# Attention output through per-head values and output weights in place of per-head value maps, in a gated cross-attention and expert block

## The reference, cut to what matters

```python
# x (4, 1024, 256) f32, context (4, 154, 192), 8 heads of 64
def attention(x, context, mask, W_q, W_k, W_v, W_o, b_o):
    q = (x @ W_q).reshape(b, n, 8, 64)
    k = (context @ W_k).reshape(b, 154, 8, 64)
    v = (context @ W_v).reshape(b, 154, 8, 64)
    sim = where(mask, einsum('bihd,bjhd->bhij', q, k) * 64 ** -0.5, max_neg)
    attn = softmax(sim, axis=-1)
    out = einsum('bhij,bjhd->bihd', attn, v).reshape(b, n, 512)
    return out @ W_o + b_o

x = x + tanh(g_xattn) * attention(layernorm(x), ...)
h = layernorm(x)
# router: 32 experts in 8 groups, the best 4 groups, the best 6 experts, weights normalised
moe = sum over the 6 experts e of weight_e * (relu(h @ up_e.T) ** 2 @ down_e.T)      # inner size 128
shared = relu(h @ shared_up.T) ** 2 @ shared_down.T                                   # inner size 512
x = x + tanh(g_ffn) * (moe + shared)
```

## Time and profile before

| | us |
|---|---|
| median of 3 runs (lowest, highest) | 1016.27 (1015.75, 1018.07) |
| profiled execution, its own time | 1015.22 |
| its span, first to last instruction | 1013.4 |
| preparation, to the first score | 0 to 63.36 |
| slots, to the last `attn_out` | 63.36 to 440.68 |
| shared experts and last routing | 440.68 to 583.03 |
| experts and final sums | 583.03 to 1013.4 |

### The profile page before, as it was taken

One profiled execution on the slowest core, in us unless ns is written; L12 is line 12 of the kernel. 1 busy time (PEld: TensorE's weight loads), 2 busy tenths in 40 slices (PEclk: granted clock), 3 DMA queues, 4 the chain that ended last, 5 costly groups with the idle time before them and its releaser, 6 DMA issues.

```text
span 1013.4 us, 16914 instructions
## 1 busy us (share of the span) xinstructions
PE 828.7 (82%) x4985; PEld 680.9 (67%) x4985; DVE 496.7 (49%) x1574; ACT 380.0 (38%) x1120; POOL 497.3 (49%) x471
## 2 busy tenths in 40 slices
PE   5879999988888898949569987988877777877873
PEld 3668888777777787625345776777766666766753
DVE  1753368586767567634411132233333465645546
ACT  1235655444444454322113143434333333343330
POOL 2112114585858585846470035554545556656551
PEclk9999999999999999989688999899989999999986
DMA  9600000122412321244155045444544789878768
GB/s 313 206 1 1 1 1 23 58 85 65 181 62 80 110 93 51 93 174 159 62 179 168 23 137 156 143 149 140 164 143 152 244 252 298 267 236 268 239 218 316
DMA packets 76712, 144.66 MB, mean 143 GB/s; under 512 B 12624, under 2 KB 57936, under 8 KB 76112
## 3 DMA queue, kind: packets, MB, share of 16 engines
q1 hardware_dynamic: 51040, 63.89, 20.8%
q0 software_dynamic: 19968, 56.52, 15.0%
q10 hardware_dynamic: 5616, 23.16, 7.4%
HBM read 73.80 MB, written 69.73 MB: 142 GB/s over the span
## 4 chain that ended last, share of the span: by engine, by line
PE 55%; DVE 14%; another core or an unknown queue 13%; issue 9%; ACT 3%; DVEq 3%; DMA 2%; POOL 0%; POOLq 0%; SPq 0%; ACTq 0%
PE ps L1224 9%; PE ps L1245 8%; PE ps L1052 5%; PE ps L1111 4%; PE ps L1208 4%; PE ps L954 4%; PE ps L1004 3%; PE ps L1099 3%; PE ps L1039 3%; PE ps L977 2%; PE ps L1234 2%; PE ps L965 2%; DVE nmax L662 1%; PE ps L995 1%
## 5 line engine op out<-in xcount | busy, mean ns | idle before, releaser
L398 POOL DMA_INDIRECT token_parts<-hid,place x224 | 221.7, 990 | 236.7 <-ACT hid L550 173.7
L385 POOL DMA_INDIRECT routed_rows<-x_n,slots x144 | 144.7, 1005 | 67.8 <-issue 41.1
L1224 PE MATMUL ps<-big,att 128*128 x896 | 131.7, 293 | 43.1 <-ACT att L536 24.5
L1052 PE MATMUL ps<-big,att 128*128 128x256 f32 x640 | 146.5, 382 | 9.9 <-ACT att L463 8.0
L1224 PEld LDWEIGHTS ps<-big,att 128*128 128x128 f32 x896 | 116.2, 202 | 56.8 <-issue 54.0
L1245 PE MATMUL ps<-big,att 128*128 x448 | 125.3, 405 | 26.3 <-ACT att L542 24.0
L1052 PEld LDWEIGHTS ps<-big,att 128*128 128x128 f32 x640 | 118.4, 190 | 28.5 <-ACT att L463 10.8
L536 ACT ACTIVATE att<-ps 128x512 f32<-128x512 f32 x112 | 67.1, 600 | 157.3 <-remote 74.3
L883 DVE TENSOR_SCALAR att<-ps 128x256 f32<-128x256 f32 x112 | 47.6, 425 | 148.5 <-PE ps L1224 87.9
L1245 PEld LDWEIGHTS ps<-big,att 128*128 128x128 f32 x448 | 81.3, 202 | 38.5 <-issue 31.4
L378 POOL TENSOR_TENSOR att<-att,rsum 128x1232 f32<-128x1232 f32 x22 | 49.5, 2249 | 94.5 <-DVE rsum L667 94.3
(11 more groups left out here) (195 smaller groups left out, 1264.4 us busy)
## 6 DMA issues: line engine op xcount, KB each, us to landing
mid<-routed_rows SPq DMA_DIRECT2D x224, 138.0 KB
big<-token_parts ACTq DMA_DIRECT2D x19, 768.0 KB
x_n<-token_parts ACTq DMA_DIRECT2D x9, 768.0 KB
routed_rows<-pad_row SPq DMA_DIRECT2D x1, 4416.0 KB
routed_rows<-pad_row SPq DMA_DIRECT2D x32, 138.0 KB
big<-in_w_moe SPq DMA_DIRECT2D x1, 4352.0 KB, 12.7
x_all<-in_x SPq DMA_DIRECT2D x4, 1024.0 KB, 13.3
token_parts<-hid,place POOLq DMA_INDIRECT x224
```

Of the source, the lines that this page charges most:

```text
L385: nc.gpsimd.indirect_dma_start(rows, bass.IndirectOffsetOnAxis(ap=slots[:, t, k:k + 1], axis=0), normed(t), None).then_inc(s_sca[b % 3], 16)
L398: nc.gpsimd.indirect_dma_start(parts, bass.IndirectOffsetOnAxis(ap=place[:, p // 2 % 4, p % 2 * 2 + j:p % 2 * 2 + j + 1], axis=0), y_sb[:, ...
L1052: ins = M(ps[:, 7, 0:D], prob_t[:, c * P:(c + 1) * P], maps_u[b][:, c, :], start=c == 0, stop=c == NCH - 1)
L1224: ins = M(ps[:, 2 + p % 2, j * P:(j + 1) * P], xt[:, p % 2, j * 256 + c * P:j * 256 + (c + 1) * P], w_exp[:, bass.ds(e, 1), c * P:(c + 1) ...
```

## The change

The maps are gone. Preparation now computes keys (8 groups) and, for each batch entry, the values `v_all[b]` in three groups: for each of the 10 chunks of 128 (head, context row) pairs and each head that has rows in it, a block of 64 columns. There are 17 such (chunk, head) pairs. The context is kept in a buffer with zeros around each entry (`ctx_w`), so that rows of other heads come out as zero. ScalarE multiplies the output weights with the gate's tanh once.

In a slot the output of a tile takes three steps: `heads_out` (17 matmuls with 64 columns, into bank 7), `scale_heads` on VectorE (the inverse of the sums, multiplied in while the 512 values leave the bank), and, a slot later, `heads_t` (4 transposes), a copy by ScalarE (`save_heads_t`), and `attn_out` (4 matmuls with 256 columns). GpSimd no longer scales anything; it adds the output bias to x. The loops have 35 slots, not 34. Queries are computed two tiles ahead, in two parts. The second norm's rows are written by ScalarE (`norm_out`), from a scale and a shift by VectorE. The first norm's statistics are computed for 8 tiles in preparation and for the other 24 inside slots 0 to 5. `normed_2_t`, `logits` and `ranks` come one or two slots later. Of the experts' weights, 20 to 31 are loaded during preparation and 0 to 19 after the last `attn_out`.

```diff
-            for T in range(NT + 11):
-                if T >= 11:
-                    scatter(T - 11)
+            def add_bias(T):
+                pool.wait_ge(s_xn1, T + 1)
+                nc.gpsimd.tensor_tensor(x_all[:, T, :], x_all[:, T, :], bias_o[:], ALU.add).then_inc(s_xb, 1)
+            for T in range(NT + 14):
                 if T < NT:
-                    normalise(T)
+                    add_bias(T)
+                if T >= 14:
+                    scatter(T - 14)
...
+            def scale_heads(T):
+                dve.wait_ge(s_avp, T + 1)
+                V.reciprocal(rsum[:, T % 2, :], esum[:, T % 4, :])
+                dve.drain()
+                if T >= 1:
+                    dve.wait_ge(s_atp, T)
+                V.tensor_tensor(att_o.rearrange("p (h d) -> p h d", h=NH), ps[:, 7, :].rearrange("p (h d) -> p h d", h=NH),
+                                rsum[:, T % 2, :].unsqueeze(2).broadcast_to([P, NH, DH]), ALU.mult).then_inc(s_scl, 1)
...
-            for T in range(NT + 2):
+            for T in range(NT + 3):
+                if T >= 3:
+                    scale_heads(T - 3)
...
+                    base = CHUNK_AT[V_GROUPS[n][0]]
+                    for ch in range(*V_GROUPS[n]):
+                        for i, h in enumerate(CHUNK_HEADS[ch]):
+                            at = CHUNK_AT[ch] - base + i * DH
+                            win = P + ch * P - h * J
+                            for c in range(2):
+                                ins = M(ps[:, bank, at:at + DH], ctx_w[:, c, b, win:win + P], wv[:, c, h * DH:(h + 1) * DH],
+                                        start=c == 0, stop=c == 1, skip_group_check=True)
...
+            def heads_out(T):
+                b = T // (NT // NB)
+                slot = T + 2
+                if T >= 1:
+                    pe.wait_ge(s_at, T)
+                if slot % 4 == 0 and slot >= 8:
+                    pe.wait_ge(s_x2t, 2 * ((slot - 8) // 4) + 1)
+                if slot % 4 == 1 and slot >= 9:
+                    pe.wait_ge(s_le, (slot - 9) // 4 + 1)
+                pe.wait_ge(s_pt, 3 * T + 3)
+                for c in range(NCH):
+                    for i, h in enumerate(CHUNK_HEADS[c]):
+                        at = CHUNK_AT[c] + i * DH
+                        ins = M(ps[:, 7, h * DH:(h + 1) * DH], prob_t[:, c * P:(c + 1) * P], v_all[b][:, at:at + DH],
+                                start=c * P <= h * J, stop=(c + 1) * P >= (h + 1) * J, skip_group_check=True)
+                ins.then_inc(s_avp, 1)
+            def heads_t(T):
+                pe.wait_ge(s_scl, T + 1)
+                for m in range(MC):
+                    ins = nc.tensor.transpose(ps[:, 7, m * P:(m + 1) * P], att_o[:, m * P:(m + 1) * P], ident)
+                ins.then_inc(s_atp, 1)
...
             def attn_out(T):
+                pe.wait_ge(s_at, T + 1)
...
-                for c in range(NCH):
-                    if c % 4 == 0:
-                        pe.wait_ge(s_pt, 3 * T + c // 4 + 1)
-                    ins = M(ps[:, 7, 0:D], prob_t[:, c * P:(c + 1) * P], maps_u[b][:, c, :], start=c == 0, stop=c == NCH - 1)
+                for m in range(MC):
+                    ins = M(ps[:, 5, 0:D], att_t[:, m * P:(m + 1) * P], wo[:, m, :], start=m == 0, stop=m == MC - 1)
                 ins.then_inc(s_av, 1)
...
-            for i, (a, b, tiles) in enumerate(((0, EARLY_1, 16), (EARLY_1, EARLY_2, 24), (EARLY_2, NE, 32))):
-                sp.wait_ge(s_av, tiles)
-                sp.dma_start(w_exp[:, a:b, :], w_moe[:, a:b, :]).then_inc(s_we[i], 16)
+            sp.dma_start(w_exp[:, EARLY:NE, :], w_moe[:, EARLY:NE, :]).then_inc(s_we[0], 16)
+            sp.wait_ge(s_av, NT)
+            sp.dma_start(w_exp[:, 0:EARLY, :], w_moe[:, 0:EARLY, :]).then_inc(s_we[1], 16)
```

More of the change, by code:

```diff
@@ L948, in normed_1_t, with queries @@
                 ins.then_inc(s_x1p, 1)
-            def queries(T):
+            def queries(T, part):
                 pe.wait_ge(s_x1t, T + 1)
-                for m in range(MC):
+                for m in (2 * part, 2 * part + 1):
                     for c in range(KC):
@@ L1077, in ranks @@
                 pe.wait_ge(s_sel, b + 1)
+                pe.wait_ge(s_x1, min(TB * b + 9, NT))
                 if b >= 1:
@@ L1131, in down_late @@
                 ins.then_inc(s_dn2, 1)
-            for T in range(NT + 2):
+            for T in range(NT + 3):
+                if T == NT + 1:
+                    for s in range(3):
+                        up(0, s)
+                if 2 <= T < NT + 2:
+                    probs_t(T - 2, 0)
+                    probs_t(T - 2, 1)
                 if T < NT:
                     scores_0(T)
-                elif T == NT + 1:
-                    for s in range(3):
-                        up(0, s)
-                if T >= 2:
-                    probs_t(T - 2, 0)
+                if T + 2 < NT:
+                    normed_1_t(T + 2)
                 if T < NT:
                     scores_1(T)
-                if T + 1 < NT:
-                    queries(T + 1)
-                if T >= 2:
-                    probs_t(T - 2, 1)
+                if T >= 3:
+                    heads_t(T - 3)
+                if 2 <= T < NT + 2:
                     probs_t(T - 2, 2)
+                if T + 2 < NT:
+                    queries(T + 2, 0)
+                if T >= 3:
+                    attn_out(T - 3)
                 if T % 4 == 0 and T >= 8:
-                    logits((T - 8) // 4)
-                if T >= 2:
-                    attn_out(T - 2)
+                    normed_2_t((T - 8) // 4, 0)
+                if T % 4 == 1 and T >= 9:
+                    logits((T - 9) // 4)
                 if T + 2 < NT:
-                    normed_1_t(T + 2)
-                if T % 4 == 3 and T >= 7:
-                    normed_2_t((T - 7) // 4, 0)
-                    normed_2_t((T - 7) // 4, 1)
-                if T % 4 == 1 and T >= 9:
-                    ranks((T - 9) // 4)
+                    queries(T + 2, 1)
+                if T % 4 == 0 and T >= 8:
+                    normed_2_t((T - 8) // 4, 1)
+                if 2 <= T < NT + 2:
+                    heads_out(T - 2)
+                if T % 4 == 3 and T >= 11:
+                    ranks((T - 11) // 4)
             up(0, 3)
+            ranks(6)
             normed_2_t(7, 0)
@@ L1195, in _ @@
             pe.wait_ge(s_row, 1)
-            for i in range(3):
+            for i in range(2):
                 pe.wait_ge(s_we[i], 16)
```

317 lines of the change are left out of this document (158 added, 159 removed).

## The result

| | before | after |
|---|---|---|
| median, us (lowest, highest; 4 runs each) | 1016.01 (1012.98, 1018.07) | 1131.41 (1128.97, 1138.79) |
| profiled execution, its span | 1013.4 | 1137.0 |
| mean granted TensorE clock | 0.941 | 0.889 |

The ratio is 1.115, 95% interval [1.11, 1.12]: slower by 115 us. The forecast was 1037 (+21), with 1014 to 1060 as its range; the sign was right and the size wrong.

The account below looks back on a forecast made before the run. TensorE was taken as the bound, busy 828.7 of 1013.4 us. Slots 3-7 +8.2, slots 8-31 +16.7, slots 0-2 -6.5, the end +11.6 and preparation -9.0 sum to +21.0, so 1037 us, range 1014 to 1060.

Parts of the forecast that it names:

- Slots 8 to 31: Routing slots: TensorE's work grows by 1.64 us a slot, waits fall from 28.5 to 7 us, +16.7 us in all.
- the 28.5 us of waits: Slots 8 to 31 of before: TensorE's idle time, 1.2 us a slot, taken as waits for other engines.
- Rival 1: Slots 8 to 31: the new cross-engine chain costs what the old waits did, 21 us more, 1058 us; chance 0.18.
- The price of the new matmuls: TensorE's 64-column float32 matmuls in `heads_out`: 0.214 us each, a floor set by two weight loads.
- Rival 3: 64-column matmuls: columns alone count, so each takes 0.108 us and the kernel 965 us; chance 0.04.
- Preparation and slots 0 to 7: Preparation 44.1 us, -9.0; slots 0 to 2 about 20 us, -6.5; slots 3 to 7 +8.2.
- The end: Behind slot 31: +15.9 us if the old hole recurs, +7.4 if not; the middle, +11.6, was taken.
- the hole of 8.5 us: End of before: VectorE waits until 449.02 though the last `attn_out` starts before 440.68; cause not in the trace.
- Rival 2: Shared-expert stretch: TensorE's 23.4 us of "issue" holes and the end's hole all go, 1009 us; chance 0.12.

Follow-up runs that it names:

- e6_plain_writes: Kernel before with four bursts of 18 plain writes issued by SyncE in slots 4, 7, 10 and 13: 846.66 us, ratio 1.000 to before at 847.
- e9_after_again: Kernel after, unchanged, run again on a chip where before took 850 us: 894.42 us, ratio 1.056 to before.
- e14_train_again: Kernel before without GpSimd's scaling of the probabilities and without a wait between tiles' row writes: 832.38 us, ratio 0.984 to before.

## Why the prediction was wrong

Lengths in us of each stretch, a slot counted from its first mask row; "no holes" takes `e6_plain_writes` as before and `e9_after_again` as after.

| | forecast difference | result: before, after | no holes: before, after |
|---|---|---|---|
| start to first score | -9.0 | 63.4, 59.2 (-4.2) | 63.0, 59.5 (-3.4) |
| slots 0-2 | -6.5 | 26.5, 18.8 (-7.7) | 27.0, 18.8 (-8.2) |
| slots 3-7 | +8.2 | 48.1, 54.9 (+6.9) | 48.1, 54.9 (+6.9) |
| slots 8-30 | +16.7 with slot 31 | 269.4, 369.9 (+100.6) | 243.1, 273.6 (+30.4) |
| slot 31 to block 7's transposes | +11.6 without slot 31 | 47.1, 75.8 (+28.7) | 40.1, 57.6 (+17.5) |
| shared stretch | 0 | 128.7, 129.8 (+1.0) | 93.8, 99.1 (+5.4) |
| experts | 0 | 430.4, 428.7 (-1.7) | 328.6, 329.4 (+0.7) |

- **Slots 8 to 31: the step that failed.** The +16.7 was made of 291.4 us of work and 7 us of waits, in place of 28.5. Measured, for one slot less, are 316.1 us of busy TensorE and 53.8 of idle: +100.6. Two readings in that step were wrong.
- **First, the scaling was counted only as work whose removal frees a wait.** That it also parted the tiles of row writes stands in no term and no rival. With it gone they form trains of 18 and 24, and slots 8 to 30 lose 100.6 - 30.4 = 70 us more than without holes. That a train does this is shown by putting it into before (1.114) and spacing it again on the same chip (1.042). For after the evidence is 1.070 in place of 1.115 when paced, on another chip. That the chip or the job has its part is shown by the same two kernels at 0.984 and 1.051.
- **Second, the 28.5 us of waits weren't there to win.** They were taken as other engines in TensorE's way, which the change would free. Without holes before has 243.14 - 235.99 = 7.2 us of them over 23 slots, so there was little to win: +30.4, not +16.7. That most of the 28.5 was a milder form of the same disturbance is inferred, not shown: of the 26.2 us in before's slots 8 to 30 only 1.8 are "issue", and most name ScalarE, VectorE or "remote"; but VectorE's and ScalarE's own "issue" time there falls from 9.4 and 12.4 us to 2.4 and 0 without holes. The new chain of waits costs next to nothing: after has 3.5 us (273.56 - 270.08).
- **Even without holes the forecast misses.** 1.056 is above the 1060/1016 = 1.043 that ended its range. The waits are the largest part of that; the later start, the shared stretch (+5.4) and the end are the rest. There nearly the whole result is TensorE's own work: its busy time grows from 782.2 to 828.6, by 46.4 us, and the span by 49.3 (of two chips; side by side the medians are 45 and 46 us apart). Rival 1's +42 lies near it, but by luck: its mechanism isn't there.
- **The price of the new matmuls: right.** 0.221 us against 0.214 forecast, slot 10.99 against 11.1. Rival 3 (columns alone) is out. By the rule of the Trainium skill (TensorE: Matmul & The Clock Gate, LDWEIGHTS) that a weight load takes its columns divided by 1.2 in ns, two loads of 128 columns are 213 ns, an estimate with which the 0.221 agrees.
- **Preparation and slots 0 to 7: right**, but for the start. Preparation lasts 59.15 - 13.95 = 45.2 us against 44.1. That a load would land 3.65 us later was missed; the sum counted only the work behind it. Slots 3 to 7 are +8.1 by the cut of the earlier trace rows (54.93 - 46.87), +6.9 by that of the table.
- **The end: the parts right, the choice wrong.** With the hole of 8.5 us in both kernels or in neither, the forecast's own sum is 15.9 and a slot's 1.6; +17.5 is what is measured without holes. It took 11.6, the middle between hole and no hole, though the hole had stood under a train of 18 writes: from 423.3 to 445.9, with VectorE waiting from 435.3 to 449.02. The rest of the 28.7 is more idle time on the chip of the result (30.7 us of TensorE against 17.2).
- **Rival 2** looked at the right thing, the "issue" holes, and said that they could grow, but priced only their going, and only in the shared stretch. There the stream is the same (+1.0); it is in the slots that they grew.

None of the versions run beats before on the chips with holes. `e14_train_again` does without them, by 1.6%, but leaves work out.

## What to carry to other kernels

When an operation is taken off an engine that also issues DMAs, ask what it kept apart: look at how many issues then stand back to back, and at what the other engines did in the old trace during the longest such train. Idle time is a wait that a new order can free only if it is still there in a run without such trains or on another chip; "issue" and "remote" as releasers are the ones to doubt first. And a float32 matmul, with its two weight loads of 128 columns, cost 0.21 to 0.24 us here whether 32, 64 or 128 columns followed.

## What the runs showed of the hardware

- On two chips (before at 1016 and 993 us), while GpSimd issued 18 or 24 indirect writes 1.27 us apart, TensorE first got nothing for 1 to 6.5 us and then instructions up to 2.5 us apart, with gaps on VectorE too. In the slots this began 6 to 7 us into the train, once 19, and lasted to the train's last 7 us or its end. On three others (847 to 850 us) trains of 24 and 48 did nothing of the kind. The physical cause stays open. The transfers themselves look the same: between 192 and 220 us the writes' packets took the same share of the DMA engines in after with holes (first) and without (second), and in the first no 16 KB load of instructions (q8) began there at all:

```profile
q0 software_dynamic: 864, 2.54, 25.5%
q14 instruction: 1, 0.01, 0.1%
...
q0 software_dynamic: 864, 2.54, 25.5%
q8 instruction: 1, 0.02, 0.3%
q14 instruction: 1, 0.01, 0.1%
```

- The cost comes twice: of the 96.4 us by which slots 8 to 30 of after are longer with holes (369.93 against 273.56), 50.3 are idle TensorE, and 46.0 are the same 2292 records taking longer, much of it at the lower level of the clock (mean 0.83 against 1.00).
- The experts' stage, equal in both kernels, took 430 us with the chip of the result and 329 without holes. One chip's time says little of another's: here the ratio itself went from 1.115 to 1.056.
